# K projection of a cross-attention loop: high and low context side by side in one 512-column matmul, the halves summed by VectorE, the bias added by GpSimd

## The chip, the cores and the metric

The kernel runs on one core of a Trainium2 chip. The metric is the device time of one execution in microseconds, as the median of three runs.

## What is computed

A two-layer perceiver block on 256 latent rows of 512 with a context of 25088 rows of 512. The part that matters here is the cross-attention of layer 1. Its keys and values are projections of the context, and its softmax runs over the queries (axis 1), separately for each key and head:

```python
K = (ctx @ Wk + bk).reshape(B, S, 16, 32)
V = (ctx @ Wv + bv).reshape(B, S, 16, 32)
scores = einsum('bihd,bjhd->bijh', Q, K) / sqrt(32)
attn = softmax(scores, axis=1)
x = einsum('bijh,bjhd->bihd', attn, V).reshape(B, S, 512) @ Wo + bo
```

Everything is float32. All 25088 context rows are used.

## The kernel before

The kernel has stages in this order: the mean over the context with part of V beside it (0 to 190 us), an attention of layer 0, a mixture of 17 experts, then the loop over the context (517 to 2216 us), another attention and a second mixture of experts. The change is in the loop alone.

Each engine runs its own program, written out as a sequence of instructions, and the programs meet at semaphores. `w.wait_ge(name, n)` makes the engine wait until semaphore `name` has reached n; `then_inc` raises it when an instruction is done. An engine takes its instructions strictly in the written order, so a wait holds up all that stands behind it on that engine.

Matmuls that need more precision than one pass of the fp32r type gives are made of three passes: each operand is split into a high part (the rounded value) and a low part (the rest), and the passes for K are, in the order of `PASSES`, high weight x high context, high weight x low context, low weight x high context.

The context comes in 98 tiles of 256 rows (index g), transposed, so that the 512 input features lie in 4 chunks (c) on 128 partitions. `CTX[:, g % 3, h, c, :]` is such a chunk; h = 0 is the high part, h = 1 the low one, 1024 elements further on. `WKV[:, 0]` and `WKV[:, 1]` are the high and low parts of the weights of K.

The loop has 784 steps k. A step handles 128 keys and one group of 4 heads: TensorE (PE) makes the scores of two heads (`scores(k, 0)`), then a block of projection, then the scores of the other two (`scores(k, 1)`). The block is a quarter of the K projection in even steps (`project_k`, line 583; `due_k(k)` names the tile g, two ahead, and the quarter ch) and a third of a V projection in most odd steps (`project_v`, line 591). After every fourth step PE does the mixing with V of four steps (`mix`, line 616).

The scores of a step lie in PSUM banks 0 and 1 (even steps) or 2 and 3 (odd steps), K's block in bank 4, V's in bank 5, the mixing in banks 6 and 7. `scores(k, half)` waits until ScalarE (ACT) has taken the exponentials of step k - 2 out of the same bank (`s_exp`).

VectorE (DVE) does in each step: the two maxima (`maxima`, line 1215), each behind its half of the scores; the reciprocals of the step before (line 1221, behind `s_exp`); in even steps `k_raw` (line 1200), which takes K's block out of bank 4 into one of the two buffers `KR[:, n % 2]` with the bias added; in some odd steps `v_out` (line 1208), which takes V out of bank 5; and in two steps of eight half a rounding of a context tile (`split_hi`, line 1178). ACT does the four exponentials of a step (line 826), each with a sum, behind the maxima.

GpSimd (POOL) does in each step: the scaling of V by the reciprocals (`scale_v`, line 1471); in odd steps `k_high` (line 1483), the rounding of K from KR to `KHL[..., 0, ...]`, behind `kr_out`; in even steps (and once in an odd one) `k_low` (line 1490), the rest; and in four steps of eight a quarter of the low context (`split_lo`, line 1463), the last of which raises `ctx_lo`.

SyncE issues the transfers. When the four quarters of K of a tile are there, `stack_k` (line 324) issues 16 transfers that stack high and low parts for the scores (`STK`), some eight steps before they are used.

`project_k` waits for `ctx_lo` of its tile, and in the loop for `kr_out`, by which bank 4 is free again. `k_raw` waits for `kp_mm` and for `kr_lo` of two quarters before, by which its KR buffer is free.

Of the kernel before, what the change touches and what calls it, by code (L numbers as in the profile page):

```python
# [10 lines left out]
ALU = mybir.AluOpType  # L11
ACT = mybir.ActivationFunctionType
AX = mybir.AxisListType

D = 512
NC = 4
NCTX = 25088
GT = 256
# [9 lines left out]
C_L0Q, C_L0K, C_L1XQ, C_L1XK, C_L1AQ, C_L1AK = 0, 4, 8, 12, 16, 20  # L28
# [14 lines left out]
wkv_hi wv_dve wv_pool wk_pool sums early_hi early_lo early_mm early_out p1_mm x_bias mean_rhs mean_mm x_mean  # L43
qk_mm qk_out av_mm av_out x_abias sc_mm sc_max sc_exp sc_rcp diag turn_mm turn_out amix_mm amix_out ao_mm x_attn
f0_xs f0_xs_act f0_hi f0_lo f0_plo f0_up f0_silu f0_mul f0_hhi f0_hlo f0_dn f0_acc gate_mm gate_sig gate_comb
ctx_hi ctx_lo kp_mm k_hi k_lo kr_out kr_hi kr_lo q_mm q_out q_split vp_mm v_out s_mm s_max s_exp s_rcp vs mix_mm ot_dve ot_act xo_mm x_xo x_xbias
f1_xs f1_xs_act f1_hi f1_lo f1_plo f1_up f1_gelu f1_hhi f1_hlo f1_dn f1_acc g1_mm g1_sub g1_exp g1_comb g1_turn g1_pt b2_mm b2_out f1_half x_lnb y_out
""".split()

# [28 lines left out]
def v_tile(n):  # L78

    return 6 * (n // 4) + n % 4  # L80
# [7 lines left out]
def due_k(k):  # L88

    return (k // 8 + 2, (k % 8) // 2) if k % 2 == 0 and k // 8 + 2 < NG else None  # L90


def due_v(k):

    n = (k + 14) // 6
    return (n, (k + 14) % 6 // 2) if k % 2 and v_tile(n) < NT else None
# [12 lines left out]
def build(nc, a):  # L109
    ctx = ExitStack()  # L110
    with ctx:
        def sb(name, shape, dt=F32, over=None):
            return (over or ctx).enter_context(nc.sbuf_tensor(name, shape, dt))
# [4 lines left out]
        BC = sb("BC", [P, 24])  # L118
# [12 lines left out]
        def bank(b, o=0, n=512):  # L131
            return PB[:, b, o:o + n]

        kv_life, ffn_life, life = ExitStack(), ExitStack(), ExitStack()
        WKV = sb("WKV", [P, 4, NC, D], F32R, kv_life)
# [17 lines left out]
        CTX = sb("CTX", [P, 3, 2, NC, GT], F32R, life)  # L153
# [4 lines left out]
        KR = sb("KR", [P, 2, GT], over=life)  # L158
# [23 lines left out]
        S = {name: ctx.enter_context(nc.semaphore(name)) for name in SEMAPHORES}  # L182
# [200 lines left out]
        def tensor_program(e):  # L383
            w = Waits(e, S)
# [17 lines left out]
            for n in range(NPAIR):  # L402
                for r in pair_v(n):
                    q, j = r // 2, 128 * (r % 2)
# [3 lines left out]
                    for z, (xh, wh) in enumerate(PASSES):  # L408
# [5 lines left out]
                        for c in range(NC):  # L414
                            w.wait_ge("wkv_hi", c + 1)
                            m = e.matmul(bank(5 + r % 3), CS[:, q % 3, xh, c, j:j + 128], WKV[:, 2 + wh, c, :],  # L416
                                         start=(z == 0 and c == 0), stop=(z == 2 and c == 3))
# [5 lines left out]
            for i in range(2):  # L423
                for c in range(NC):
                    m = e.matmul(bank(2 + i), XT[:, c, 128 * i:128 * i + 128], w0[:, 0, c, :],
                                 start=(c == 0), stop=(c == NC - 1))
                m.then_inc(S["p1_mm"], 1)
            w.wait_ge("mean_rhs", 1)
            for c in range(NC):
                m = e.matmul(bank(4), SBC[:, c, :], w0[:, 1, c, :], start=(c == 0), stop=(c == NC - 1))  # L430
# [139 lines left out]
            for i in range(2):  # L570
                for c in range(NC):
                    m = e.matmul(bank(3, 16 * i, 16), XT[:, c, 128 * i:128 * i + 128], gw0[:, c, :],
                                 start=(c == 0), stop=(c == NC - 1))
# [9 lines left out]
            def project_k(g, ch, kb=4):  # L583
                w.wait_ge("ctx_lo", g + 1)
                for z, (wh, xh) in enumerate(PASSES):
                    for c in range(NC):
                        m = e.matmul(bank(kb, 0, GT), WKV[:, wh, c, 128 * ch:128 * ch + 128], CTX[:, g % 3, xh, c, :],  # L587
                                     start=(z == 0 and c == 0), stop=(z == 2 and c == 3))
                m.then_inc(S["kp_mm"], 1)

            def project_v(n, part):
                t = v_tile(n)
                g, j = t // 2, 128 * (t % 2)
                if part == 0:
                    w.wait_ge("ctx_lo", g + 1)
                    if n:
                        w.wait_ge("v_out", n)
                xh, wh = PASSES[part]
                for c in range(NC):
                    m = e.matmul(bank(5), CTX[:, g % 3, xh, c, j:j + 128], WKV[:, 2 + wh, c, :],  # L600
                                 start=(part == 0 and c == 0), stop=(part == 2 and c == 3))
                if part == 2:
                    m.then_inc(S["vp_mm"], 1)

            def scores(k, half):
                t, c = k // 4, k % 4
                g, j = t // 2, 128 * (t % 2)
                w.wait_ge(f"d_s{g % 2}", 256 * (g // 2 + 1))
                if k >= 2:
                    w.wait_ge("s_exp", 2 * (k - 2) + half + 1)  # L610
                for s in (2 * half, 2 * half + 1):
                    m = e.matmul(bank(2 * (k % 2) + half, 256 * (s % 2), 256), STK[:, g % 2, s, c, j:j + 128],  # L612
                                 QS[:, s, c, :], start=True, stop=True)
                m.then_inc(S["s_mm"], 1)

            def mix(k):
                t, c, b = k // 4, k % 4, k % RING
                w.wait_ge("vs", k + 1)
                for s in range(4):
                    m = e.matmul(  # L620
                        PB[32 * s:32 * s + 32, 6 + c // 2, 256 * (c % 2):256 * (c % 2) + 256],
                        VS[:, b, 32 * s:32 * s + 32], EE[:, b, s, :],
                        start=(t == 0 and c % 2 == 0), stop=(t == NT - 1), skip_group_check=True)
                m.then_inc(S["mix_mm"], 1)
# [6 lines left out]
            for c4 in range(NC):  # L631
                for c in range(NC):
                    m = e.matmul(bank(2 + c4, 0, 256), wqx[:, c, 128 * c4:128 * c4 + 128], XT[:, c, :],
                                 start=(c == 0), stop=(c == NC - 1))
# [5 lines left out]
            for n in range(2):  # L640
                for part in range(3):
                    project_v(n, part)
            project_v(*due_v(-1))
            w.wait_ge("k_lo", 8)
            w.wait_ge("d_q", 256)
            for k in range(NCH):
                scores(k, 0)
                if due_k(k):
                    g, ch = due_k(k)
                    if k:  # L650
                        w.wait_ge("kr_out", 4 * (g - 2) + ch)
                    project_k(g, ch)
                elif due_v(k):
                    project_v(*due_v(k))
                scores(k, 1)
                if k % MIX == MIX - 1:
                    for n in range(max(k - MIX - 1, 0), k - 1):
                        mix(n)
# [5 lines left out]
            for i in range(2):  # L664
                for c in range(NC):
                    m = e.matmul(bank(2 + i), OT[:, c, 128 * i:128 * i + 128], WO[:, c, :],
                                 start=(c == 0), stop=(c == NC - 1))
# [42 lines left out]
            for n in range(128):  # L710
                up1(n)
                if n == 1:
                    wait_xt(5)
                    w.wait_ge("d_b1", 16)
                    for i in range(2):
                        for c in range(NC):
                            m = e.matmul(bank(7, 8 * i, 8), XT[:, c, 128 * i:128 * i + 128], gw1[:, c, :],
                                         start=(c == 0), stop=(c == NC - 1))
# [4 lines left out]
                if n == 4:  # L723
                    w.wait_ge("g1_comb", 1)
                    for i in range(2):
                        m = e.transpose(PB[0:8, 6, 128 * i:128 * i + 128], comb1[:, i, :], ident[:, :])
# [152 lines left out]
        def vector_program(e):  # L879
            w = Waits(e, S)  # L880
# [24 lines left out]
            for c in (0, 2, 3):  # L905
                z = slice(512 * c, 512 * c + 512)
# [3 lines left out]
            for n in range(NPAIR + 1):  # L910
                if n < NPAIR:
# [3 lines left out]
                        axis=AX.X, op=ALU.add).then_inc(S["sums"], 1)  # L915
# [284 lines left out]
            def k_raw(g, ch):  # L1200
                n = 4 * (g - 2) + ch
                w.wait_ge("kp_mm", 4 * g + ch + 1)
                if n >= 2:
                    w.wait_ge("kr_lo", n - 1)
                e.tensor_scalar(KR[:, n % 2, :], bank(4, 0, GT), BC[:, C_L1XK + ch:C_L1XK + ch + 1], None,  # L1205
                                ALU.add).then_inc(S["kr_out"], 1)

            def v_out(n):
                t = v_tile(n)
# [46 lines left out]
            for k in range(NCH):  # L1256
                maxima(k, 0)
                maxima(k, 1)
                if k >= 1:
                    reciprocals(k - 1)  # L1260
                if due_k(k):
                    k_raw(*due_k(k))
                if due_v(k) and due_v(k)[1] == 2:
                    v_out(due_v(k)[0])
                if k % 8 in (2, 3) and k // 8 + 3 < NG:
                    split_hi(k // 8 + 3, (k % 2,))
# [105 lines left out]
        def gpsimd_program(e):  # L1372
            w = Waits(e, S)
# [35 lines left out]
            for n in range(NPAIR):  # L1409
                for r in pair_v(n)[0:2:2]:  # L1410
                    q = r // 2
                    g = 3 * q + 2
# [7 lines left out]
                if n in (12, 15, 18, 21):  # L1420
                    c = (n - 12) // 3
                    z = slice(512 * c, 512 * c + 512)
# [60 lines left out]
            def k_high(g, ch):  # L1483
                n = 4 * (g - 2) + ch
                w.wait_ge("kr_out", n + 1)
                if ch == 0:
                    w.wait_ge(f"d_s{g % 2}", 256 * (g // 2))
                e.tensor_copy(KHL[:, g % 2, 0, ch, :], KR[:, n % 2, :]).then_inc(S["kr_hi"], 1)  # L1488

            def k_low(g, ch):  # L1490
# [47 lines left out]
        @block.tensor  # L1538
        def _(e):
            tensor_program(e)  # L1540
# [78 lines left out]
```

## Time and profile before

| | |
|---|---|
| median of three runs | 2662.23 us (2661.63 to 2662.91) |
| the profiled execution, its own time | 2662.88 us |
| its span, from the first to the last instruction | 2661.2 us |
| mean granted clock of TensorE | 0.992 of full |
| instructions | 59615 |
| bytes read from and written to HBM | 244.47 MB, 17.30 MB |

The trace gives each instruction a start and a duration. PE is TensorE's matmul, PEld its weight load, which runs beside the matmuls before it. A matmul's recorded duration is its latency: in a row of matmuls the next one starts long before the last has ended, so what one costs is read from start to start. The columns of a timeline row are start in us, duration in us, engine, line, operation, tiles, shape and count; rows of one kind that follow each other are merged into one, with their number behind x.

### The profile page before, as it was taken

To read this page: it belongs to the slowest core of one execution; us is meant where nothing else is said; L and a number is where in the kernel's file an instruction comes from. 1 tells how busy PE (TensorE), PEld (TensorE's weight loads), DVE (VectorE), ACT (ScalarE), POOL (GpSimd) and SP (SyncE) were. 2 spreads that over 40 slices of the span, in tenths; PEclk is the share of its full clock that TensorE was granted. 3 is DMA by queue.
4 is the path that set the end of the run, shared out by engine and by line. 5 is a ranking of instruction groups with operands and counts; after the bars stand their busy time and mean duration, and the time that the engine had idled before them with its cause. 6 is when DMAs were issued, how large, how long until landed. Compare 5 with 4: busy or idle time off the path is not lost.

```text
span 2661.2 us, 59615 instructions
## 1 busy us (share of the span) xinstructions
PE 2608.1 (98%) x21096; PEld 2202.5 (83%) x21096; DVE 1971.5 (74%) x3890; ACT 1862.7 (70%) x6826; POOL 1272.0 (48%) x2199
## 2 busy tenths in 40 slices
PE   8998999899999999999999999999999998999998
PEld 6875999788888888888888888888888885799997
DVE  8876866577787777787777787777787776655555
ACT  2213444288888888888888888888888886355553
POOL 4532111165655565655665655656655653222222
PEclk9998999999999999999999999999999999999999
DMA  9992554556666656666666666666666652545451
GB/s 385 388 396 97 196 190 167 135 154 182 157 161 173 164 157 160 165 162 167 161 166 158 158 169 168 160 158 168 154 164 168 167 130 109 187 177 190 184 190 72
DMA packets 132301, 473.34 MB, mean 178 GB/s; under 512 B 31128, under 2 KB 31256, under 8 KB 124832
## 3 DMA queue, kind: packets, MB, share of 16 engines
q1 hardware_dynamic: 122400, 451.69, 57.9%
q10 hardware_dynamic: 9600, 17.83, 1.8%
q8 instruction: 166, 2.72, 0.4%
q14 instruction: 135, 1.11, 0.1%
HBM read 244.47 MB, written 17.30 MB: 98 GB/s over the span
## 4 chain that ended last, share of the span: by engine, by line
PE 95%; DVE 2%; ACT 1%; DMA 1%; issue 0%; POOL 0%; ACTq 0%; SPq 0%; DVEq 0%; POOLq 0%
PE PB L587 21%; PE PB L612 15%; PE PB L620 14%; PE PB L600 14%; PE PB L688 7%; PE PB L703 6%; PE PB L416 6%; PE PB L549 6%; PE PB L562 3%; PE PB L445 1%; PE PB L476 1%; DMA AR<-in_ctx 1%; ACT EE L832 1%; PE PB L452 1%; PE PB L497 0%
## 5 line engine op out<-in xcount | busy, mean ns | idle before, releaser
L832 ACT ACTIVATE EE<-PB,small 128x256 f32<-128x256 f32 x3136 | 1445.1, 482 | 204.8 <-DVE small L1217 191.4
L1217 DVE TENSOR_REDUCE small<-PB 128x2 f32<-128x512 f32 x1568 | 1031.5, 682 | 355.3 <-PE PB L612 355.1
L832 ACT ACTIVATION_READ_ACCUMULATOR EE<-PB,small 128x1 f32 x3136 | 665.0, 212 | 0.0
L1478 POOL TENSOR_TENSOR VS<-V,small 128x128 f32<-128x128 f32 x784 | 320.5, 409 | 689.4 <-DVE small L1223 682.1
L587 PE MATMUL PB<-CTX,WKV 128*128 128x256 f32 x4704 | 624.7, 282 | 3.1 <-POOL CTX L1466 3.1
L587 PEld LDWEIGHTS PB<-CTX,WKV 128*128 128x128 f32 x4704 | 588.1, 190 | 3.4 <-POOL CTX L1466 3.3
L612 PEld LDWEIGHTS PB<-QS,STK 128*128 128x128 f32 x3136 | 469.1, 190 | 122.0 <-issue 79.9
L612 PE MATMUL PB<-QS,STK 128*128 128x256 f32 x3136 | 555.1, 288 | 5.3 <-ACT EE L832 5.2
L600 PE MATMUL PB<-WKV,CTX 128*128 128x512 f32 x1584 | 433.9, 396 | 3.0 <-DVE V L1213 3.0
L620 PE MATMUL PB<-EE,VS 128*32 128x256 f32 x6272 | 381.4, 384 | 0.0
L600 PEld LDWEIGHTS PB<-WKV,CTX 128*128 128x128 f32 x1584 | 274.0, 191 | 40.0 <-DVE V L1213 3.9
L1493 POOL TENSOR_TENSOR KHL<-KR,KHL 128x256 fp32r<-128x256 f32 x384 | 299.8, 781 | 7.7
L1466 POOL TENSOR_TENSOR CTX<-RAW,CTX 128x256 fp32r<-128x256 f32 x384 | 289.2, 753 | 29.1 <-DVE CTX L1185 29.1
L620 PEld LDWEIGHTS PB<-EE,VS 128*32 128x32 f32 x6272 | 184.4, 110 | 128.5 <-issue 2.1
L1527 POOL TENSOR_TENSOR HS<-HF,HS 128x256 fp32r<-128x256 f32 x128 | 101.5, 793 | 265.5 <-DVE HS L1293 265.5
L416 PE MATMUL PB<-WKV,CS 128*128 128x512 f32 x768 | 177.3, 392 | 10.4 <-ACT CS L756 10.0
L863 ACT ACTIVATE HF<-PB,MS 128x256 f32<-128x256 f32 x128 | 61.0, 477 | 178.5 <-PE PB L688 178.4
L416 PEld LDWEIGHTS PB<-WKV,CS 128*128 128x128 f32 x768 | 144.8, 189 | 42.0 <-ACT CS L756 10.4
L1205 DVE TENSOR_SCALAR KR<-PB,BC 128x256 f32<-128x256 f32 x384 | 174.3, 454 | 0.1
L549 PEld LDWEIGHTS PB<-XS,WS 128*128 128x128 f32 x1224 | 152.8, 194 | 3.6 <-issue 1.1
L549 PE MATMUL PB<-XS,WS 128*128 128x256 f32 x1224 | 153.9, 285 | 0.8 <-ACT XS L783 0.8
L1488 POOL CAST KHL<-KR 128x256 fp32r<-128x256 f32 x384 | 152.6, 397 | 0.0
(201 smaller groups left out, 2546.3 us busy)
## 6 DMA issues: line engine op xcount, KB each, us to landing
STK<-KHL SPq DMA_DIRECT2D x1568, 128.0 KB, 2.5
RW<-in_l1f SPq DMA_DIRECT2D x32, 2048.0 KB, 8.1
AR<-in_ctx SPq DMA_DIRECT2D x49, 1024.0 KB, 8.5
RAW<-in_ctx SPq DMA_DIRECT2D x98, 512.0 KB, 3.7
WF<-in_l0f SPq DMA_DIRECT2D x17, 2304.0 KB, 8.9
v_scr<-RAW ACTq DMA_DIRECT2D x64, 256.0 KB, 7.6
V<-v_scr SPq DMA_DIRECT2D x64, 256.0 KB, 2.9
WA<-in_l0a SPq DMA_DIRECT2D x1, 4096.0 KB, 13.9
```

The lines of the kernel that those rows point to most:

```text
L416: m = e.matmul(bank(5 + r % 3), CS[:, q % 3, xh, c, j:j + 128], WKV[:, 2 + wh, c, :], start=(z == 0 and c == 0), stop=(z == 2 and c == 3))
L549: m = e.matmul(bank(k, 256 * u, 256), wt[:, c, 128 * k:128 * k + 128], XS[:, xh, c, :], start=(z == 0 and c == 0), stop=(z == 2 and c == 3))
L587: m = e.matmul(bank(kb, 0, GT), WKV[:, wh, c, 128 * ch:128 * ch + 128], CTX[:, g % 3, xh, c, :], start=(z == 0 and c == 0), stop=(z == 2 a ...
L600: m = e.matmul(bank(5), CTX[:, g % 3, xh, c, j:j + 128], WKV[:, 2 + wh, c, :], start=(part == 0 and c == 0), stop=(part == 2 and c == 3))
L612: m = e.matmul(bank(2 * (k % 2) + half, 256 * (s % 2), 256), STK[:, g % 2, s, c, j:j + 128], QS[:, s, c, :], start=True, stop=True)
L620: m = e.matmul(PB[32 * s:32 * s + 32, 6 + c // 2, 256 * (c % 2):256 * (c % 2) + 256], VS[:, b, 32 * s:32 * s + 32], EE[:, b, s, :], start= ...
L688: m = e.matmul(bank(n % 4, 0, 256), w1[:, c, 128 * f:128 * f + 128], XS1[:, xh, c, :], start=(z == 0 and c == 0), stop=(z == 2 and c == 3))
L832: m = e.activation(EE[:, b, s, :], bank(2 * (k % 2) + half, 256 * (s % 2), 256), ACT.Exp, bias=nm[:, b, s:s + 1], accum_out=su[:, b, s:s + 1])
L1217: e.tensor_reduce(nm[:, k % RING, 2 * half:2 * half + 2], bank(2 * (k % 2) + half).rearrange("p (s i) -> p s i", s=2), axis=AX.X, op=ALU.m ...
L1466: m = e.tensor_tensor(CTX[:, g % 3, 1, c, :], RAW[:, g % 3, GT * c:GT * c + GT], CTX[:, g % 3, 0, c, :].bitcast(F32), ALU.subtract)
L1478: e.tensor_tensor(VS[:, b, :].rearrange("p (s d) -> p s d", s=4), V[:, t % 4, 128 * c:128 * c + 128].rearrange("p (s d) -> p s d", s=4), r ...
L1493: e.tensor_tensor(KHL[:, g % 2, 1, ch, :], KR[:, n % 2, :], KHL[:, g % 2, 0, ch, :].bitcast(F32), ALU.subtract).then_inc(S["kr_lo"], 1)
```

## The change

K's block in the loop is made of 8 matmuls instead of 12. The high weights of a chunk are multiplied with high and low context in one matmul of 512 columns, which writes both halves of bank 4; then the low weights are multiplied with the high context, 256 columns, onto the first half. `k_raw` becomes a reduce over the two halves, without the bias. POOL adds the bias in place in KR, ahead of `k_high`, and waits for its own result (new semaphore `kr_bias`). The two tiles that are projected ahead of the loop stay as they were.

```diff
+            def project_k_wide(g, ch):
+                w.wait_ge("ctx_lo", g + 1)
+                if g >= 2 and (g, ch) != (2, 0):
+                    w.wait_ge("kr_out", 4 * (g - 2) + ch)
+                z = slice(128 * ch, 128 * ch + 128)
+                for c in range(NC):
+                    e.matmul(bank(4).rearrange("p (h j) -> p h j", h=2), WKV[:, 0, c, z], CTX[:, g % 3, :, c, :],
+                             start=(c == 0), stop=False)
+                for c in range(NC):
+                    m = e.matmul(bank(4, 0, GT), WKV[:, 1, c, z], CTX[:, g % 3, 0, c, :], start=False, stop=(c == NC - 1))
+                m.then_inc(S["kp_mm"], 1)
+
@@ tensor_program, the loop
                 if due_k(k):
-                    g, ch = due_k(k)
-                    if k:
-                        w.wait_ge("kr_out", 4 * (g - 2) + ch)
-                    project_k(g, ch)
+                    project_k_wide(*due_k(k))
@@ vector_program, k_raw
-                e.tensor_scalar(KR[:, n % 2, :], bank(4, 0, GT), BC[:, C_L1XK + ch:C_L1XK + ch + 1], None,
-                                ALU.add).then_inc(S["kr_out"], 1)
+                e.tensor_reduce(KR[:, n % 2, :], bank(4).rearrange("p (h j) -> p j h", h=2), axis=AX.X,
+                                op=ALU.add).then_inc(S["kr_out"], 1)
@@ gpsimd_program, k_high
                     w.wait_ge(f"d_s{g % 2}", 256 * (g // 2))
+                e.tensor_scalar(KR[:, n % 2, :], KR[:, n % 2, :], BC[:, C_L1XK + ch:C_L1XK + ch + 1], None,
+                                ALU.add).then_inc(S["kr_bias"], 1)
+                w.wait_ge("kr_bias", n + 1)
                 e.tensor_copy(KHL[:, g % 2, 0, ch, :], KR[:, n % 2, :]).then_inc(S["kr_hi"], 1)
```

## Rows read from the trace of the kernel before

**Rows 1.** Page, part 1: busy us, share of the span, instructions of each engine.
```profile
PE 2608.1 (98%) x21096; PEld 2202.5 (83%) x21096; DVE 1971.5 (74%) x3890; ACT 1862.7 (70%) x6826; POOL 1272.0 (48%) x2199
```
**Rows 2.** Page, part 4: shares of the chain that ended last, by line.
```profile
PE PB L587 21%; PE PB L612 15%; PE PB L620 14%; PE PB L600 14%; PE PB L688 7%; PE PB L703 6%; PE PB L416 6%; PE PB L549 6%; PE PB L562 3%; PE PB L445 1%; PE PB L476 1%; DMA AR<-in_ctx 1%; ACT EE L832 1%; PE PB L452 1%; PE PB L497 0%
```
**Rows 3.** Windows, the loop: PE, PEld, DVE, ACT, POOL busy; clock, DMA share, GB/s.
```profile
520.00:2200.00 1680.00, 1676.86 (x15415) 1403.88 (x15416) 1326.65 (x3025) 1483.13 (x6186) 998.56 (x1923) 1.00 0.63 161
```
**Rows 4.** Timeline of PE, four steps of the loop.
```profile
1502.70 1.59 PE L587 MATMUL PB<-CTX,WKV 128*128 128x256 f32 x12
1504.13 0.64 PE L612 MATMUL PB<-QS,STK 128*128 128x256 f32 x4
1504.61 1.09 PE L600 MATMUL PB<-WKV,CTX 128*128 128x512 f32 x4
1505.54 0.63 PE L612 MATMUL PB<-QS,STK 128*128 128x256 f32 x4
1506.01 1.60 PE L587 MATMUL PB<-CTX,WKV 128*128 128x256 f32 x12
...
1511.38 0.40 PE L587 MATMUL PB<-CTX,WKV 128*128 128x256 f32 x2
```
**Rows 5.** Timeline of PE from 100 us, ahead of the loop.
```profile
99.73 25.55 PE L416 MATMUL PB<-WKV,CS 128*128 128x512 f32 x112
```
**Rows 6.** Timeline of DVE, the same steps as in rows 4.
```profile
1505.26 0.45 DVE L1205 TENSOR_SCALAR KR<-PB,BC 128x256 f32<-128x256 f32 x1
...
1506.91 0.66 DVE L1213 TENSOR_TENSOR V<-PB,BI 128x512 f32<-128x512 f32 x1
...
1508.77 0.45 DVE L1205 TENSOR_SCALAR KR<-PB,BC 128x256 f32<-128x256 f32 x1
```
**Rows 7.** Timeline of PE's weight loads, the same steps.
```profile
1505.89 1.50 PEld L587 LDWEIGHTS PB<-CTX,WKV 128*128 128x128 f32 x12
1507.32 0.55 PEld L612 LDWEIGHTS PB<-QS,STK 128*128 128x128 f32 x4
1507.80 0.78 PEld L600 LDWEIGHTS PB<-WKV,CTX 128*128 128x128 f32 x4
```
**Rows 8.** Groups by line: busy us, mean ns of one, idle before, releaser.
```profile
L1217 DVE TENSOR_REDUCE small<-PB 128x2 f32<-128x512 f32 x1568 | 1031.5, 682 | 355.3 <-PE PB L612 355.1
L913 DVE TENSOR_REDUCE small<-AR 128x8 f32<-128x2048 f32 x49 | 110.3, 2276 | 2.0 <-DMA AR<-in_ctx 2.0
...
L932 DVE TENSOR_REDUCE small<-small 128x4 f32<-128x392 f32 x1 | 0.8, 844 | 0.0
```
**Rows 9.** Timeline just ahead of the loop, a weight load that waits for DVE.
```profile
515.84 0.69 DVE L1213 TENSOR_TENSOR V<-PB,BI 128x512 f32<-128x512 f32 x1 [4.70 <-PE PB L600]
...
516.58 0.76 PEld L600 LDWEIGHTS PB<-WKV,CTX 128*128 128x128 f32 x4 [1.22 <-DVE V L1213]
```
**Rows 10.** Timeline of ACT, the last part of step 1's first exponentials.
```profile
1507.17 0.20 ACT L832 ACTIVATION_READ_ACCUMULATOR EE<-PB,small 128x1 f32 x1
```
**Rows 11.** Groups by line of POOL, then the timeline around `ctx_lo` and its K block.
```profile
L1493 POOL TENSOR_TENSOR KHL<-KR,KHL 128x256 fp32r<-128x256 f32 x384 | 299.8, 781 | 7.7
...
L1488 POOL CAST KHL<-KR 128x256 fp32r<-128x256 f32 x384 | 152.6, 397 | 0.0
...
1404.77 0.40 POOL L1478 TENSOR_TENSOR VS<-V,small 128x128 f32<-128x128 f32 x1 [0.30 <-DVE small L1223]
...
1405.82 0.74 POOL L1466 TENSOR_TENSOR CTX<-RAW,CTX 128x256 fp32r<-128x256 f32 x1
...
1407.11 1.50 PEld L587 LDWEIGHTS PB<-CTX,WKV 128*128 128x128 f32 x12
```
**Rows 12.** Timeline of SyncE's queue and PE's weight loads: last stacking, first use.
```profile
2001.99 5.68 SPq L331 DMA_DIRECT2D STK<-KHL  x9
...
2014.48 0.30 PEld L612 LDWEIGHTS PB<-QS,STK 128*128 128x128 f32 x2 [0.41 <-issue]
```

More of the change, by code:

```diff
@@ L45 @@
 f0_xs f0_xs_act f0_hi f0_lo f0_plo f0_up f0_silu f0_mul f0_hhi f0_hlo f0_dn f0_acc gate_mm gate_sig gate_comb
-ctx_hi ctx_lo kp_mm k_hi k_lo kr_out kr_hi kr_lo q_mm q_out q_split vp_mm v_out s_mm s_max s_exp s_rcp vs mix_mm ot_dve ot_act xo_mm x_xo x_xbias
+ctx_hi ctx_lo kp_mm k_hi k_lo kr_out kr_bias kr_hi kr_lo q_mm q_out q_split vp_mm v_out s_mm s_max s_exp s_rcp vs mix_mm ot_dve ot_act xo_mm x_xo x_xbias
 f1_xs f1_xs_act f1_hi f1_lo f1_plo f1_up f1_gelu f1_hhi f1_hlo f1_dn f1_acc g1_mm g1_sub g1_exp g1_comb g1_turn g1_pt b2_mm b2_out f1_half x_lnb y_out
```

## The prediction

> **What bounds the kernel now.** I read the busy shares first: PE 98%, DVE 74%, ACT 70%, POOL 48% [rows 1]. An average like this does not say who decides in one stage, so the chain of waits comes next: 21% of the span lies on PE's line 587, the K projection that is changed, with the other lines of the same loop (612, 620, 600) behind it [rows 2]. The stretch that holds the loop confirms it: PE is busy for 1676.86 of 1680 us, while DVE has 1326.65, ACT 1483.13 and POOL 998.56 [rows 3]. So the loop runs at PE's rate, at full granted clock, and everything else has to stay hidden behind PE. Then I read PE's own order of work. It repeats: one K block starts at 1502.70, the block two further on at 1511.38, so four steps of the loop with two K blocks take 8.68 us [rows 4]. There are 384 K blocks in the loop, 192 such pairs.
>
> Call the steps of a pair 0, 1, 2, 3. K blocks stand in steps 0 and 2, V blocks in 1 and 3.
>
> **PE's part.** A K block takes 1504.13 - 1502.70 = 1.43 us for 12 matmuls of 256 columns, 0.119 each [rows 4]. The new block has 4 matmuls of 512 columns and 4 of 256. A V block is 4 matmuls of 512: 1505.54 - 1504.61 = 0.93, or 0.2325 each [rows 4]. New block: 0.93 + 4 x 0.119 = 1.406, a gain of 0.024 us. The columns streamed are the same, 3072 both times; only four weight loads and the fixed part of four instructions go, and they were almost wholly beside the matmuls. The best rate of 512 columns in the trace is 25.55 / 112 = 0.228 [rows 5], which makes the gain 0.041. The worst is no gain, since the moving operand now comes in two runs of 256 that lie apart, which no row shows. I take 0.024: at most 384 x 0.024 = 9 us, between 0 and 16.
>
> **DVE's part.** `k_raw` reads 256 values per partition from PSUM in 0.45 us [rows 6]; the reduce that replaces it reads 512 and adds them in pairs, the two of a pair 1024 bytes apart. Lower end: the reduce of the score maxima also reads 512 from PSUM, side by side, in 0.682 us [rows 8]; fewer cycles than elements are not to be seen in any reduce here. Upper end: a reduce that steps through memory instead of reading side by side. There is one, line 932: 392 elements with four elements from one to the next take 0.844 us [rows 8]. The unstrided reduce of line 913 takes 2.276 us for 2048 and line 1217 0.682 for 512, so a contiguous element costs (2.276 - 0.682) / 1536 = 0.00104 us and the fixed part is 0.15 [rows 8]. For line 932 that leaves (0.844 - 0.15) / 392 = 0.00177 per element, 1.7 times as much, with no idle time before it. Carried to 512 elements: 0.15 + 0.906 = 1.056 us. If each element cost two contiguous ones, 0.15 + 1.065 = 1.215. I take 1.056, since the pattern, not the count, is what is new here, and line 932 is the only row with such a pattern; it reads SBUF and not PSUM, which is the weak point. In the Trainium skill (Advanced Engine Details and Errata, Memory Cachelines) PSUM has lines of two FP32 values and access to a different line each time is said to be slower; the rows on SBUF agree with the like rule there, no row shows it for PSUM. The Trainium skill also speaks for the other side: the table in VectorE: DVE Perf Modes (The TRN2 errata) gives PSUM to SBUF as 120 cycles plus one per element at 0.96 GHz, whatever the pattern. By it the reduce would take about 0.66 us and the sum would be that of the first rival.
>
> **What the longer instruction runs into.** Bank 4 has one owner at a time: the K block of step 2 waits for `kr_out` of step 0. `k_raw` starts at 1505.26 and ends at 1505.71 [rows 6]; the weight load of the next K block starts at 1505.89 [rows 7]. That is a margin of 0.18. A wait of PE for DVE costs 0.05: an instruction of DVE ended at 516.53, the weight load that waited for it began at 516.58 [rows 9]. Left: 0.13. The new reduce takes 0.60 more, so PE stands still for 0.47 us in each pair, and this wait takes the place of nothing: it is new. The next two waits have about the same margin. The V block of step 3 waits for `v_out`, 1506.91 + 0.66 = 1507.57 against 1507.80 [rows 6, 7], 0.23 less 0.05. The scores of step 3 wait for the exponentials of step 1, which are behind the maxima that stand behind `k_raw` on DVE: the last of ACT ends at 1507.37 [rows 10], the third weight load of the group at 1507.32 + 0.24 = 1507.56 [rows 7], 0.19 less 0.05 = 0.14. ACT and DVE are 0.60 late there, PE itself 0.47 - 0.024 = 0.45; 0.60 - 0.14 - 0.45 = 0.01 us more. The reduce in step 2 delays nobody: the next K block follows over 2 us later (1508.77 + 0.45 against the block at 1511.38, [rows 4, 6]), and DVE gets a stretch without work before the next group.
>
> Sum of a pair: 0.47 + 0.01 - 2 x 0.024 = +0.43 us; 192 x 0.43 = 83 us. A weight load stands 0.12 ahead of its matmul (1505.89 and 1506.01, [rows 4, 7]), so one that comes a little late need not delay the matmul by as much; I take 3 us off for that: +80. The profiled execution takes 2662.88 (span 2661.2), 0.65 over the median of 2662.23: 2662.2 + 80 = **2742 us**.
>
> **POOL's part** costs nothing in this sum. The bias adds one instruction with one tensor input, and a wait for its own result. Lower end for the instruction: the cast of the same tile, 0.40; upper end: the two-input subtraction, 0.78 [rows 11]. With the wait 0.45 to 0.83. Behind it on POOL stand `k_high`, the low half of the context and the scaled V, for which PE's K, the stacking transfers and the mix wait. The tightest is `ctx_lo`: its last part ends at 1405.82 + 0.74 = 1406.56, the K block that needs it loads at 1407.11 [rows 11]: 0.55 less 0.05, and POOL stood idle for 0.30 before 1404.77 behind the only bias that comes between. 0.80 of cover against 0.45 to 0.83. Without this cover each 0.1 us would cost 96 x 0.1 = 10 us, as one context tile serves two pairs. The stacking transfers start later by the same half microsecond; the last of them is issued at 2007.67 and first needed at 2014.48 [rows 12]. KR's two buffers are freed two K blocks ahead of their use.
>
> **Rivals.** First: the reduce reads at full rate, 0.682. Speaks for it: every PSUM read of DVE in the profile runs at one element per cycle, and 512 of them are two plain runs. Against it: line 932. The instruction is 0.23 longer: 0.10 at K, 0.23 - 0.14 - (0.10 - 0.024) = 0.01 at the scores, less 0.048: +0.06 us a pair, 12 us, less the 4 for late weight loads: **2670**. The change would then be nearly neutral, with PE's gain given back in the same loop.
> Second, on the other side (not slower): the reduce at 0.682, 512 columns at 0.228, and the 0.12 between a weight load and its matmul absorbing the late release of bank 4 nearly in full. Then the pair has no stall at K, 0.03 at the scores, and gains 2 x 0.041: -0.05 us, -10 us, **2653**. It decides as soon as the stalls of a pair are below twice the gain of a block, which with the plain margins of 0.13 and 0.14 needs a reduce under 0.65 us. Against it: three waits in a row have that margin, and all three must give.
> Third: POOL becomes the bound, if the bias with its wait takes over 0.8 us; at 1.2 us it is 0.4 x 96 = 38 us on top of the first rival, **2708**. Against it: POOL has 40% of the loop free [rows 3].
> Fourth: the change does not do what it says, because 512 columns in two runs stream slower than in one. At 0.25 each a block takes 1.48, 0.05 more than now; that adds 384 x 0.07 = 28 us to whichever case holds.
>
> **Chances.** Forecast (a slowed strided read, 1.0 to 1.22 us) 0.55, its own range 2725 to 2775. First rival 0.25, second 0.10, third 0.04, fourth 0.06. The range that holds 8 in 10 has to take in the first rival: 2664 to 2775. About 5 us, 0.2%, is what a measurement of this kernel tells from no change. Slower by more: the forecast, the third and fourth, and over half of the first rival, 0.77. Within: the rest of the first and some of the second, 0.16. Faster: 0.07.
>
> **What would show it.** Line 1214's reduce (KR<-PB, 128x256 from 128x512) at about 1.06 us: right; at 0.68: the first rival. PE's weight loads of the K line should show idle time released by DVE KR, once per pair, of 0.4 to 0.5 us; the K block itself should shrink from 1.43 to 1.41; the loop's PE busy share should fall to some 95%. PE idle before the K line with POOL's CTX as the releaser would speak for the third. The forecast is wrong if the reduce takes under 0.75 us, or if it takes 1.06 and PE shows no wait for it.

## The result and the profile after

The changed kernel takes 2693.02 us in the median of four runs (2691.54 to 2694.38) against 2661.93 in four runs of the kernel before: 1.0117 times as long, 95% interval 1.0104 to 1.0129. That is slower, as forecast, but by 31 us and not by 80, and for the most part for another reason. The profiled execution took 2691.54 us, 28.7 more than that of before.

The line numbers have moved. In the changed kernel the K block is lines 597 (512 columns) and 600 (256), the V block 612, the scores 624, the mix 632. On DVE the rounding of the context is 1194, `k_raw` 1214, the maxima 1226, the reciprocals 1232; ACT's exponentials are 841. On POOL the low context is 1475, the scaling of V 1487, the bias 1497, `k_high` 1500, `k_low` 1505. (Before, 600 was the V block and 612 the scores.)

First the page of the changed kernel, parts 1, 4 and 5. They answer to [rows 1, 2, 8, 11]. In part 4, "issue" is time in which an engine waited for nothing that the profile shows.

```profile
PE 2631.6 (98%) x19560; PEld 2140.9 (80%) x19560; DVE 2060.7 (77%) x3890; ACT 1863.1 (69%) x6826; POOL 1632.9 (61%) x2583
...
PE 60%; POOL 22%; DVE 13%; issue 3%; ACT 1%; DMA 1%; ACTq 0%; SPq 0%; POOLq 0%; DVEq 0%
...
L1497 POOL TENSOR_SCALAR KR<-KR,BC 128x256 f32<-128x256 f32 x384 | 363.5, 947 | 0.0
...
L597 PEld LDWEIGHTS PB<-CTX,WKV 128*128 128x128 f32 x1536 | 259.4, 188 | 61.5 <-POOL CTX L1475 25.9
...
L1214 DVE TENSOR_REDUCE KR<-PB 128x256 f32<-128x512 f32 x384 | 256.1, 667 | 0.3 <-issue 0.3
```

PE's share of busy time is 98% as before and hides the loss: a matmul that waits is recorded long (below, the group of four at 1504.62, which waits, has 1.17 us, the one at 1501.34 has 1.09). The chain shows it: 60% on PE, 22% on POOL, 13% on DVE. The same line of the kernel before:

```profile
PE 95%; DVE 2%; ACT 1%; DMA 1%; issue 0%; POOL 0%; ACTq 0%; SPq 0%; DVEq 0%; POOLq 0%
```

Two numbers contradict the working of the prediction. The reduce takes 0.667 us, not 1.056. The bias on POOL takes 0.947 us, above the upper end of 0.78.

The second view is PE's timeline with the weight loads of the K line, from one K block that waits to the next. They answer to [rows 4, 7].

```profile
1501.34 1.09 PE L597 MATMUL PB<-CTX,WKV 128*128 128x512 f32 x4
1502.27 0.63 PE L600 MATMUL PB<-CTX,WKV 128*128 128x256 f32 x4
1502.74 0.64 PE L624 MATMUL PB<-QS,STK 128*128 128x256 f32 x4
1503.22 1.09 PE L612 MATMUL PB<-WKV,CTX 128*128 128x512 f32 x4
1504.14 0.63 PE L624 MATMUL PB<-QS,STK 128*128 128x256 f32 x4
...
1504.58 0.76 PEld L597 LDWEIGHTS PB<-CTX,WKV 128*128 128x128 f32 x4
1504.62 1.17 PE L597 MATMUL PB<-CTX,WKV 128*128 128x512 f32 x4
...
1510.34 0.76 PEld L597 LDWEIGHTS PB<-CTX,WKV 128*128 128x128 f32 x4 [0.36 <-POOL CTX L1475]
```

An undisturbed K block takes 1502.74 - 1501.34 = 1.40 us, against 1.43. The gain is there. At 1504.58 the next block begins 0.05 after `k_raw` (below): that is the wait for bank 4. Over steps 104 to 695 this distance is 0.05 us on average in steps 2 and 6 of eight, and 0.18 in the kernel before. The list of waits has no line for it, though the prediction had named one (PEld released by DVE KR) as its sign. At 1510.34 the block of the next tile waits 0.36 us for POOL's low context. The same stretch on DVE and POOL (they answer to [rows 6, 11]):

```profile
1499.46 0.96 DVE L1194 CAST CTX<-RAW 128x512 fp32r<-128x512 f32 x1
1500.35 1.27 DVE L1226 TENSOR_REDUCE small<-PB 128x2 f32<-128x512 f32 x2
1501.55 0.16 DVE L1232 RECIPROCAL small<-small 128x4 f32<-128x4 f32 x1
...
1503.87 0.66 DVE L1214 TENSOR_REDUCE KR<-PB 128x256 f32<-128x512 f32 x1
```
```profile
1499.41 0.73 POOL L1505 TENSOR_TENSOR KHL<-KR,KHL 128x256 fp32r<-128x256 f32 x1
...
1501.79 0.49 POOL L1487 TENSOR_TENSOR VS<-V,small 128x128 f32<-128x128 f32 x1 [1.64 <-DVE small L1232]
1502.26 0.92 POOL L1497 TENSOR_SCALAR KR<-KR,BC 128x256 f32<-128x256 f32 x1
1503.25 0.40 POOL L1500 CAST KHL<-KR 128x256 fp32r<-128x256 f32 x1
1503.62 0.74 POOL L1475 TENSOR_TENSOR CTX<-RAW,CTX 128x256 fp32r<-128x256 f32 x1
1504.32 0.40 POOL L1487 TENSOR_TENSOR VS<-V,small 128x128 f32<-128x128 f32 x1
1504.67 0.75 POOL L1505 TENSOR_TENSOR KHL<-KR,KHL 128x256 fp32r<-128x256 f32 x1
1505.38 0.74 POOL L1475 TENSOR_TENSOR CTX<-RAW,CTX 128x256 fp32r<-128x256 f32 x1
1506.08 0.40 POOL L1487 TENSOR_TENSOR VS<-V,small 128x128 f32<-128x128 f32 x1
1506.46 0.92 POOL L1497 TENSOR_SCALAR KR<-KR,BC 128x256 f32<-128x256 f32 x1
1507.45 0.40 POOL L1500 CAST KHL<-KR 128x256 fp32r<-128x256 f32 x1
...
1509.56 0.74 POOL L1475 TENSOR_TENSOR CTX<-RAW,CTX 128x256 fp32r<-128x256 f32 x1
```

POOL has no idle time from 1501.79 until the last part of the low context ends at 1510.30, and PE's weight load follows 0.04 later. Two biases, at 1502.26 and 1506.46, stand in this row, each 0.99 from its start to that of the cast behind it. `k_raw` ends at 1503.87 + 0.66 = 1504.53.

To see where the 31 us lie I took, of each kernel's trace, the mean distance in ns between the first score matmuls of successive steps, for steps 104 to 695, by the place of the step in a tile of eight. Step 0 is the one with the first K block of a tile, the block that waits for `ctx_lo`. A stall that shows up late in a step can fall in the next one.

| kernel | 0 | 1 | 2 | 3 | 4 | 5 | 6 | 7 | sum |
|---|---|---|---|---|---|---|---|---|---|
| before | 2008 | 1407 | 1907 | 3359 | 2008 | 1407 | 1907 | 3359 | 17362 |
| after | 2267 | 1404 | 1942 | 3367 | 1975 | 1405 | 1941 | 3370 | 17671 |
| no_bias | 1980 | 1405 | 1942 | 3373 | 1979 | 1405 | 1942 | 3373 | 17399 |
| pool_alone | 2235 | 1407 | 1907 | 3359 | 2007 | 1407 | 1907 | 3359 | 17588 |
| wide_alone | 1981 | 1407 | 1880 | 3359 | 1981 | 1407 | 1880 | 3359 | 17254 |
| ctx_first | 1981 | 1407 | 1938 | 3374 | 1981 | 1407 | 1938 | 3374 | 17400 |
| raw_first | 2448 | 1403 | 1878 | 3444 | 1978 | 1403 | 1878 | 3443 | 17875 |
| both_orders | 1972 | 1406 | 1878 | 3435 | 1972 | 1406 | 1878 | 3437 | 17384 |
| tt_bias | 1975 | 1406 | 1940 | 3366 | 1976 | 1411 | 1950 | 3360 | 17384 |
| late_recip | 1973 | 1405 | 1875 | 3758 | 1973 | 1406 | 1874 | 3830 | 18094 |
| before_late_recip | 2419 | 1407 | 1907 | 3471 | 2010 | 1407 | 1907 | 3359 | 17887 |

After less before is 0.309 us a tile, 98 tiles: 30 us, so the loop explains all of it. Step 0 alone has +0.259.

### The profile page after: what moved, and what is told of

It is laid out like the page before. It is cut to its first block, busy times and chain, and to the rows that moved or that the text cites. A ratio compares the mean times of both kernels' runs of the same rounds, so it can differ in the third digit from the quotient of the medians.

```text
span 2689.8 us, 56927 instructions
## 1 busy us (share of the span) xinstructions
PE 2631.6 (98%) x19560; PEld 2140.9 (80%) x19560; DVE 2060.7 (77%) x3890; ACT 1863.1 (69%) x6826; POOL 1632.9 (61%) x2583
## 4 chain that ended last, share of the span: by engine, by line
PE 60%; POOL 22%; DVE 13%; issue 3%; ACT 1%; DMA 1%; ACTq 0%; SPq 0%; POOLq 0%; DVEq 0%
PE PB L597 8%; PE PB L624 7%; PE PB L697 7%; PE PB L712 6%; POOL CTX L1475 6%; PE PB L416 6%; PE PB L612 6%; POOL KR L1497 6%; PE PB L549 6%; DVE small L1226 5%; PE PB L632 5%; POOL KHL L1505 4%; POOL VS L1487 4%; PE PB L600 3%; PE PB L562 3%
## 5 line engine op out<-in xcount | busy, mean ns | idle before, releaser
L597 PE MATMUL PB<-CTX,WKV 128*128 128x512 f32 x1536 | 442.0, 409 | 8.5 <-POOL CTX L1475 7.5
L1497 POOL TENSOR_SCALAR KR<-KR,BC 128x256 f32<-128x256 f32 x384 | 363.5, 947 | 0.0
L597 PEld LDWEIGHTS PB<-CTX,WKV 128*128 128x128 f32 x1536 | 259.4, 188 | 61.5 <-POOL CTX L1475 25.9
L1475 POOL TENSOR_TENSOR CTX<-RAW,CTX 128x256 fp32r<-128x256 f32 x384 | 283.5, 738 | 29.0 <-DVE CTX L1194 29.0
L1505 POOL TENSOR_TENSOR KHL<-KR,KHL 128x256 fp32r<-128x256 f32 x384 | 294.4, 767 | 8.2
L600 PEld LDWEIGHTS PB<-CTX,WKV 128*128 128x128 f32 x1536 | 234.3, 189 | 33.4
L1214 DVE TENSOR_REDUCE KR<-PB 128x256 f32<-128x512 f32 x384 | 256.1, 667 | 0.3 <-issue 0.3
L600 PE MATMUL PB<-CTX,WKV 128*128 128x256 f32 x1536 | 243.3, 280 | 0.0
```

Of the source, the lines that this page charges most:

```text
L597: e.matmul(bank(4).rearrange("p (h j) -> p h j", h=2), WKV[:, 0, c, z], CTX[:, g % 3, :, c, :], start=(c == 0), stop=False)
L600: m = e.matmul(bank(4, 0, GT), WKV[:, 1, c, z], CTX[:, g % 3, 0, c, :], start=False, stop=(c == NC - 1))
L1475: m = e.tensor_tensor(CTX[:, g % 3, 1, c, :], RAW[:, g % 3, GT * c:GT * c + GT], CTX[:, g % 3, 0, c, :].bitcast(F32), ALU.subtract)
L1497: e.tensor_scalar(KR[:, n % 2, :], KR[:, n % 2, :], BC[:, C_L1XK + ch:C_L1XK + ch + 1], None, ALU.add).then_inc(S["kr_bias"], 1)
L1505: e.tensor_tensor(KHL[:, g % 2, 1, ch, :], KR[:, n % 2, :], KHL[:, g % 2, 0, ch, :].bitcast(F32), ALU.subtract).then_inc(S["kr_lo"], 1)
```

## The experiments

Theory A was: two waits, one behind each longer instruction. The bias delays `ctx_lo` (about 28 us), the reduce delays bank 4 (about 11), and the shorter K block gives 9 back. Theory B, the rival: DVE's longer instruction is at the root, and POOL only shows it. Ratios are to the kernel before, with 95% intervals; the last run, strides, is a single execution that was read for four durations alone. In the edits, ... stands for text that is left out, and some lines are shortened.

**no_bias.** The change without the instruction on POOL; K's bias is left out.

```diff
-                e.tensor_scalar(KR[:, n % 2, :], KR[:, n % 2, :], BC[...], None, ALU.add).then_inc(S["kr_bias"], 1)
-                w.wait_ge("kr_bias", n + 1)
```

> The changed kernel without POOL's bias instruction and its wait (K's bias is left out; K block of 8 matmuls and DVE's reduce stay). Theory A: the bias (0.95 us on POOL, twice ahead of ctx_lo in a tile) makes the K block of every eighth step wait about 0.29 us, 96 times, 28 us of the 31 lost; the reduce (0.66 us) costs some 11 us by the wait for bank 4 and the shorter K block gives 9 back. Then this kernel takes 2664 to 2667 us. Theory B: the longer DVE instruction is the main cost, directly or by what it delays, and POOL's late ctx_lo only stands in for it; then it stays at 2685 to 2693.

2666.11 us, 1.0012 (1.0003 to 1.0020). Theory A holds: with the same reduce of 0.668 us, 27 us are gone, and in the table only step 0 differs from after by more than 0.01. B falls, here and in the next run.

**pool_alone.** The kernel before with the bias instruction and its wait; the bias is added twice.

```diff
+                e.tensor_scalar(KR[:, n % 2, :], KR[:, n % 2, :], BC[...], None, ALU.add).then_inc(S["kr_bias"], 1)
+                w.wait_ge("kr_bias", n + 1)
                 e.tensor_copy(KHL[:, g % 2, 0, ch, :], KR[:, n % 2, :]).then_inc(S["kr_hi"], 1)
```

> The kernel before with nothing but the bias instruction and its wait added on POOL (the bias is added twice to K). Theory A: ctx_lo has 0.53 us of margin and 0.30 of idle time ahead of it against about 1.0 us, so the K block waits 0.15 to 0.29 us per tile: 2677 to 2690. Theory B: 2662 to 2665, as DVE's instruction is the old one.

2683.79 us, 1.0078 (1.0064 to 1.0092): 21 us of the 31 from this instruction alone. In the table it is again step 0 and nothing else, +0.227. The list of waits puts this wait down to "issue" (95 times) and not to CTX, but the trace leaves no doubt: in each of the 74 tiles of steps 104 to 695 the weight load of the K block starts 0.11 us after the end of the last low context, in the kernel before 0.55 to 0.75 after it. In the full change the same wait costs 2267 - 1980 = 0.287 a tile. The other 0.06 comes from one tile in three, in which DVE's reciprocals are late (see POOL's part below); no run has the bias with the reduce alone or with the new K block alone, so their shares in it are not separated.

**wide_alone.** The kernel before with the new K block alone (`project_k_wide` as in the change). `k_raw` stays the old instruction and reads the first half of bank 4, and POOL is as before, so the product of high weight and low context is made and then left out.

```diff
                 if due_k(k):
-                    g, ch = due_k(k)
-                    if k:
-                        w.wait_ge("kr_out", 4 * (g - 2) + ch)
-                    project_k(g, ch)
+                    project_k_wide(*due_k(k))
```

> The 8-matmul K block alone: DVE takes out the first half with the bias as before (the product of high weight and low context is left out), POOL as before. Both theories: 0.024 us less per K block, 384 blocks: 2653 (2651 to 2658). If 512 columns in two runs were slow, 2662 or more.

2653.23 us, 0.9960 (0.9948 to 0.9973), so a gain of 10 us, 0.027 in each of four steps of the table. no_bias differs from it only by the reduce in the place of the old instruction (0.668 for 0.455 us): 12.9 us more, in steps 2 and 6 (+0.062) and 3 and 7 (+0.014), as the first rival's working placed it.

**ctx_first.** The full change with POOL's order turned in even steps.

```diff
+                if 3 <= k % 8 <= 6 and k // 8 + 3 < NG:
+                    split_lo(k // 8 + 3, (k % 8 - 3,))
                 if k % 8 in (2, 4, 6) and due_k(k - 2):
                     k_low(*due_k(k - 2))
-                if 3 <= k % 8 <= 6 and k // 8 + 3 < NG:
-                    split_lo(k // 8 + 3, (k % 8 - 3,))
```

> The changed kernel with POOL's quarter of the low context ahead of the low half of K in even steps (k_low), nothing left out. ctx_lo comes 0.7 us earlier. Theory A: the wait of 0.29 us per tile goes, 2664 to 2668. Theory B: no change, 2690 to 2695.

2665.98 us, 1.0011 (1.0002 to 1.0021). Nothing is left out and the bias takes as long as ever, but its delay no longer reaches PE. The wait list of the two kernels, the same line of each (total in us, times, longest):

```profile
PEld PB L597 <- POOL CTX L1475: 25.9, 96, 3.3
```
```profile
PEld PB L597 <- POOL CTX L1475: 3.3, 1, 3.3
```

The first is the change: once per tile. The second is ctx_first; the one wait left is the first tile's, which the kernel before has too.

**tt_bias.** The full change with the bias as a two-input addition.

```diff
-                e.tensor_scalar(KR[:, n % 2, :], KR[:, n % 2, :], BC[:, ...:... + 1], None, ALU.add)
+                e.tensor_tensor(KR[:, n % 2, :], KR[:, n % 2, :], BC[:, ...:... + 1].to_broadcast([P, GT]), ALU.add)
```

> The changed kernel with the bias as a two-input addition of a broadcast column on POOL, a form that takes 0.74 to 0.78 us for this size instead of 0.95. Two such stand ahead of ctx_lo in a tile, so the 0.29 us of waiting shrinks by 0.2 (one) to 0.29 (both, with the reciprocals' wait in between): 2665 to 2674 us. If POOL's instruction time were not the cause: 2693.

2665.55 us, 1.0013 (1.0004 to 1.0022). The instruction is quicker than expected, and the whole wait is gone (step 0: 1975). Its group in part 5:

```profile
L1497 POOL TENSOR_TENSOR KR<-KR,BC 128x256 f32<-128x256 f32 x384 | 234.8, 611 | 0.0
```

**raw_first** and **both_orders.** DVE's `k_raw` between the two maxima of an even step, where DVE waits for PE; alone, and with ctx_first.

```diff
                 maxima(k, 0)
+                if due_k(k):
+                    k_raw(*due_k(k))
                 maxima(k, 1)
                 if k >= 1:
                     reciprocals(k - 1)
-                if due_k(k):
-                    k_raw(*due_k(k))
```

> The changed kernel with DVE's new place of k_raw alone, POOL's order as in the change. Theory: the wait for bank 4 (0.06 us in steps 2 and 6 of eight, 0.01 in 3 and 7) goes, the wait for ctx_lo stays or shrinks a little as the reciprocals come no later: 2676 to 2684. If DVE alone had been the cause: 2655.

2711.18 us, 1.0183 (1.0169 to 1.0197). The wait for bank 4 goes, as expected (steps 2 and 6: 1878, as short as in wide_alone). But the time rises by 18 us over the change. "The reciprocals come no later" was wrong: in an even step they stand behind the reduce now, POOL's step begins with them, and the wait for `ctx_lo` grows (step 0: 2448, from 2267). Nearly as much lies in steps 3 and 7 (3444 and 3443, from 3367 and 3370), which the next run takes up. The same line of its wait list:

```profile
PEld PB L597 <- POOL CTX L1475: 41.4, 96, 2.8
```

> The changed kernel, nothing left out, with POOL's low context ahead of k_low as in the run ctx_first, and on DVE k_raw right behind the first maximum of an even step, ahead of the second one. DVE stands idle there for 0.5 to 1 us behind PE, so the reduce ends before the wait for bank 4 begins. Theory (two waits behind two longer instructions, and nothing else): both waits go and the gain of the shorter K block, 0.027 us x 384, is left: 2651 to 2656, under the kernel before. If the reduce costs through what DVE does in total, or the maxima that now stand behind it come too late for ACT: 2662 to 2670.

2666.07 us, 1.0013 (1.0004 to 1.0022), not 2653. Both waits named are gone, but steps 3 and 7 have 3435 for 3359. PE and DVE of both_orders, then its ACT, then two rows of the kernel before:

```profile
1506.29 1.08 PE L597 MATMUL PB<-CTX,WKV 128*128 128x512 f32 x4
...
1507.88 0.69 DVE L1214 TENSOR_REDUCE KR<-PB 128x256 f32<-128x512 f32 x1 [0.70 <-PE PB L600]
1508.49 0.68 DVE L1226 TENSOR_REDUCE small<-PB 128x2 f32<-128x512 f32 x1
...
1509.17 1.26 DVE L1226 TENSOR_REDUCE small<-PB 128x2 f32<-128x512 f32 x2
```
```profile
1509.21 0.48 ACT L841 ACTIVATE EE<-PB,small 128x256 f32<-128x256 f32 x1 [0.97 <-DVE small L1226]
...
1510.12 0.47 ACT L841 ACTIVATE EE<-PB,small 128x256 f32<-128x256 f32 x1
```
```profile
1505.63 1.28 DVE L1217 TENSOR_REDUCE small<-PB 128x2 f32<-128x512 f32 x2
...
1506.35 0.47 ACT L832 ACTIVATE EE<-PB,small 128x256 f32<-128x256 f32 x1
```

The K block of this pair starts at 1506.29 in both_orders, at 1502.70 in the kernel before. DVE is at the next step's maxima 2.88 us later, no later than before (1505.63 against 1502.70, 2.93). But the maximum of step 0's second half now comes late, so its exponentials start 2.92 us after the block and hold ACT until 1510.12. In the kernel before, those of step 1 start 1506.35 - 1502.70 = 3.65 after the block; now 3.83. That is 0.18, more than the 0.14 of margin of [rows 7, 10]. The loop bears it out: in all 148 steps 3 and 7 of the window the weight load of the scores starts 0.05 us after the last exponential that it needs, in the kernel before 0.19. So the second alternative of this expectation came true: the maxima are too late for ACT.

**before_both_orders.** The same two new orders in the kernel before.

> The kernel before with both new orders and nothing else: a control. PE waits for neither of the two there, so 2661 to 2665 us; a gain would mean that the orders and not the change pay in the run both_orders.

2661.93 us, 1.0000 (0.9991 to 1.0010). The orders alone neither cost nor gain.

**late_recip** and **before_late_recip.** The reciprocals of odd steps moved behind the next odd step's first maximum; in the change with tt_bias and ctx_first, and alone in the kernel before.

```diff
                 maxima(k, 0)
+                if k % 2 and k >= 3:
+                    reciprocals(k - 2)
                 maxima(k, 1)
-                if k >= 1:
+                if k % 2:
                     reciprocals(k - 1)
```

> The changed kernel, nothing left out, with the bias as a two-input addition, POOL's low context ahead of k_low, and on DVE the reciprocals of an odd step moved behind the first maximum of the next odd step, so that neither the reduce nor the maximum behind it has them in front (0.085 us earlier each). Theory (two short margins behind k_raw, 0.13 and 0.14 us, against 0.21 of longer reduce): the wait at bank 4 goes and the one for the exponentials shrinks to 0.03 or less per pair, so 0.03 of the 0.056 us gain per pair is left, 192 pairs: 2655 to 2660. If DVE's total work or POOL's later start decides instead: 2664 or more.

> The kernel before with the later reciprocals alone, a control: 2661 to 2664, as no engine in front of PE is late there.

2734.78 us, 1.0275 (1.0261 to 1.0289), and 2713.53 us, 1.0195 (1.0181 to 1.0209). Both expectations failed by far, the control's too. The wait list of the control, four of its lines:

```profile
POOL VS L1480 <- DVE small L1223: 627.4, 364, 2.4
...
PEld PB L620 <- POOL VS L1480: 37.3, 112, 0.5
...
PEld PB L587 <- issue: 29.5, 84, 0.5
PE PB L587 <- POOL CTX L1468: 8.5, 28, 0.3
```

POOL's whole step hangs on the reciprocals, and these come 1.0 to 1.4 us later in even steps. In the control the larger part is `ctx_lo` again: step 0 has +0.411, and the K block's weight load starts 0.11 us after the last low context in every tile, as in pool_alone. The rest is the mix (line 620), which waits for the scaled V: step 3 has +0.112. In late_recip the earlier low context keeps step 0 short (1973), and all of the loss lies in steps 3 and 7, at the mix, where its list has 166 waits for the scaled V. So an instruction of 0.17 us that comes about 1 us later costs 52 us in a kernel whose POOL was idle 40% of the loop.

**strides.** Three more reduces of the 392 partial sums, behind line 932 (941 here).

```diff
             e.tensor_reduce(csum, sums.rearrange("p (g c) -> p c g", c=NC), ...)
+            e.tensor_reduce(small[:, 416:420], sums.rearrange("p (c g) -> p c g", c=NC), ...)
+            e.tensor_reduce(small[:, 420:424], sums.rearrange("p (g c) -> p c g", c=NC), ...)
+            e.tensor_reduce(small[:, 424:620], sums.rearrange("p (h j) -> p j h", h=2), ...)
```

> The changed kernel with three more DVE reduces of the 392 partial sums in SBUF behind the one of line 932, their results unused: side by side in four rows of 98, again stepped by four, and in pairs that lie 196 elements apart. The prediction carried the stepped rate (0.00177 us per element) over to PSUM. If the step across memory is what is slow in SBUF: 0.55, 0.84 and 0.84 us. If pairs read in turn from two runs are as quick as in PSUM: the third takes 0.55. If line 932 was slow for another reason (its place): all three 0.55.

DVE's timeline of this one execution:

```profile
188.66 0.85 DVE L941 TENSOR_REDUCE small<-small 128x4 f32<-128x392 f32 x1
189.54 0.56 DVE L943 TENSOR_REDUCE small<-small 128x4 f32<-128x392 f32 x1
190.14 0.85 DVE L945 TENSOR_REDUCE small<-small 128x4 f32<-128x392 f32 x1
191.03 0.56 DVE L947 TENSOR_REDUCE small<-small 128x196 f32<-128x392 f32 x1
```

A step of four elements is slow in SBUF (0.85), twice over. Pairs read in turn from two runs are as quick as side by side (0.56). The pattern of the change is the second, and the row that the forecast carried over was of the first.

## Why the prediction was right or wrong, by its steps

**PE's part: right.** 0.024 us per K block was forecast, 0.027 measured (wide_alone), 10 us for 9. Two runs of 256 columns streamed no slower than one of 512 (four matmuls in 0.93 us from 1501.34, the V block's in 0.92 from 1503.22).

**DVE's part: wrong, and with it the forecast.** The failed step is "I take 1.056, since the pattern, not the count, is what is new here, and line 932 is the only row with such a pattern". Line 932 had another pattern, and 0.667 was measured, just under the lower end of 0.682 and under the 0.75 that the prediction had named as its sign of being wrong. The wait at bank 4 was mis-sized with it: 0.47 us a pair was forecast, 0.062 measured. Of the two sentences on the Trainium skill, the one on lines (Advanced Engine Details and Errata, Memory Cachelines) did not bear on this reduce: its pairs lie in different lines, in PSUM and in the run strides in SBUF, and neither read was slowed. The Trainium skill's table (VectorE: DVE Perf Modes, The TRN2 errata) gives 0.66 for this instruction, and it came out at that (median 0.661).

**What the longer instruction runs into: right in place and order.** Bank 4 first, the exponentials of step 1 second. With the measured 0.213 us more, the working gives 0.213 - 0.13 = 0.08 at bank 4 and 0.01 to 0.02 at the scores, less the 0.02 a pair (4 us) that it took off for late weight loads. 0.062 + 0.014 = 0.076 was measured, 12.9 us between no_bias and wide_alone. That the difference is due to the weight loads no run shows by itself.

**POOL's part: wrong, and the largest term.** The sum put it at nothing, and it cost 27 us. "0.80 of cover against 0.45 to 0.83" failed first by the size of the instruction: it was bounded by the cast and the two-input subtraction, 0.40 to 0.78, and took 0.947, with its wait 0.99. The cover was nearly right: 0.99 - 0.80 = 0.19 us a tile, against 0.227 in pool_alone. There the first bias of a tile (step 3) is absorbed, and POOL still waits 0.53 to 0.69 us for the reciprocals of step 4; the second (step 5) reaches `ctx_lo`.

The rest the prediction did not see: it took POOL's steps to begin when they did before. In the window the changed kernel has two kinds of tiles. In 49 of 74 POOL still has a pause of 0.31 to 0.49 us in step 4, the first bias is absorbed, and step 0 takes 2.20 us, 0.22 more than in no_bias. In the other 25, every third tile, the pause is gone, both biases reach `ctx_lo`, and step 0 takes 2.39. The tile of the rows above is of the second kind. The rounding at 1499.46 takes 0.96 us there (0.39 to 0.61 in the loop before), two reduces follow, and the reciprocal at 1501.55 comes 0.55 after the scores that follow the mix (1501.00); in the kernel before it comes 0.30 to 0.50 ahead of them. The next tile of the same trace is of the first kind; its pause, and its shorter wait of PE:

```profile
1521.82 0.40 POOL L1487 TENSOR_TENSOR VS<-V,small 128x128 f32<-128x128 f32 x1 [0.46 <-DVE small L1232]
```
```profile
1527.94 0.76 PEld L597 LDWEIGHTS PB<-CTX,WKV 128*128 128x128 f32 x4 [0.17 <-POOL CTX L1475]
```

Third rival: right in mechanism and place (step 0 of a tile, CTX as releaser, 96 times); its rule of 0.1 us to 10 us gives 0.19 x 96 = 18 us for 0.99, and 27 were measured. It had 0.04 of the chance.

**The sum** with measured terms: -10 for the K block, +13 for bank 4 and the exponentials, +27 for `ctx_lo`, 30 of the 31 us. The first and third rivals hold together; their sum (2708) was priced only for a bias of 1.2 us. The time lies inside the stated 2664 to 2775, but by luck: the range was drawn to hold the forecast and the first rival, and between 2670 and 2725 lay only the third (2708) and, as 2670 + 28, the fourth, with 0.10 of the chance together.

No version of the change here that keeps the whole computation beats the kernel before: ctx_first, tt_bias and both_orders end 0.1% above it. The 10 us of the K block are paid back by 0.21 us more of `k_raw`, at bank 4 and the scores in ctx_first, at the exponentials in both_orders.

## What to carry to other kernels

An instruction that joins an engine with 40% of its time free can still cost: count the unbroken row of instructions from what releases that engine to what another one waits for, and ask whether the releaser itself comes later after the change. Read several repeats of the loop and not one: here every third tile lost 0.41 us and the others 0.22. Take an unknown duration from an instruction of the same form, operands and pattern, and when there is none, widen the bounds beyond the nearest rows on the engine concerned. A wait of this kind can often be taken away by order alone: 27 us went with two lines of POOL's program in another order, the duration untouched.

## What the hardware showed that was not expected

On POOL an addition of a per-partition scalar to 128x256 float32 took 0.947 us, the same addition with the column broadcast as a second tensor 0.611, a cast 0.397, and a two-input subtraction of full tensors 0.735 to 0.782. Of the additions and the subtraction, the one with a single tensor operand was the slowest. On DVE a reduce that reads pairs from two runs, 256 apart in PSUM or 196 in SBUF, ran at the rate of a contiguous one; stepping by four elements in SBUF cost 0.85 for 0.56 us. DVE's rounding of 128x512 in SBUF took 0.39 to 0.61 us in the loop before. In the loop of the change 25 of 148 took 0.96 to 0.97, in no_bias 75 of 150 took 0.94 to 0.97, in tt_bias 100 of 150 took 0.83 to 0.96. Each of these 200 began 0.05 to 0.08 us after the start of a subtraction or addition of POOL and ended 0.28 us after that one's end, whether it took 0.61 or 0.74. Why these differ no run here tells.
